# A transformer layer pair in float32: fillings for TensorE, and up projections from high and low parts

## What is computed

```python
x  = x + layernorm(attn(layernorm(x)))        # 16 heads of 16, rotary, window of 250, causal
y  = layernorm(x)                             # the second block:
z  = rmsnorm(y + attn2(y), n1)                # 16 heads, no mask, keys and values through 64 columns
shared = swiglu(z @ W_shared_in) @ W_shared_out        # 256 -> 2*512 -> 256
h      = swiglu(z @ W1_shared)                         # 256 -> 2*512
out = z + shared + sum over 8 experts of (h @ W2[e]) * w[:, e]   # top 2 of a group by a gate
x  = x + layernorm(rmsnorm(out, n2))
```

## Time and profile before

| | us |
|---|---|
| median of 3 runs | 2344.89 |
| lowest, highest | 2335.24, 2353.25 |
| profiled execution | 2316.51 |
| its span, first to last instruction | 2314.5 |
| batches 1 to 7, each (stages A to the next A) | 265.6 to 279.9 |
| batch 0 (from its A) | 239.4 |

### The profile page before, as it was taken

The page is one execution under the profiler, slowest core; times in us unless marked ns, Lnnn a source line. Parts: engine busy times, 40 slices in busy tenths (PEclk is TensorE's granted clock), DMA queues, the critical chain, the costliest instruction groups (busy, mean ns, idle before and its releaser), DMA issues.

```text
span 2314.5 us, 31755 instructions
## 1 busy us (share of the span) xinstructions
PE 2060.3 (89%) x9200; PEld 1089.0 (47%) x9200; DVE 1386.8 (60%) x4293; ACT 829.0 (36%) x1713; POOL 341.5 (15%) x647
## 2 busy tenths in 40 slices
PE   6868899998999999999899989989899998999986
PEld 4343445535364453635436353453635545354455
DVE  6457455755756466674556756575565656747454
ACT  2434424262432424334242542325233262423410
POOL 3323112101220003100031011210112101210000
PEclk8577889998998988999789998898899899889988
DMA  4003002110030101101021010211002010020212
GB/s 166 2 28 138 1 2 92 37 38 10 6 133 1 48 1 73 66 2 48 1 83 55 7 42 1 90 49 38 11 2 101 37 38 10 6 89 35 77 52 91
DMA packets 23083, 104.64 MB, mean 45 GB/s; under 512 B 3312, under 2 KB 14192, under 8 KB 18288
## 3 DMA queue, kind: packets, MB, share of 16 engines
q1 hardware_dynamic: 21168, 89.81, 10.7%
q0 software_dynamic: 1728, 12.58, 1.4%
HBM read 84.56 MB, written 16.78 MB: 44 GB/s over the span
## 4 chain that ended last, share of the span: by engine, by line
PE 70%; DVE 19%; issue 7%; ACT 3%; DMA 0%; POOL 0%; DVEq 0%; SPq 0%; POOLq 0%; ACTq 0%
PE fb L732 13%; PE fb L710 11%; PE sm L644 10%; PE ot L684 10%; PE st L670 5%; PE st L629 3%; PE st L613 3%; DVE negmax L1011 2%; DVE acc L1199 2%; DVE stats L925 2%; PE dn L652 2%; PE dn L696 2%; PE dn L613 2%; PE sm L670 1%; DVE sm L1008 1%
## 5 line engine op out<-in xcount | busy, mean ns | idle before, releaser
L535 ACT ACTIVATE probs<-st 128x512 f32<-128x512 f32 (+3 forms) x832 | 404.9, 506 | 472.9 <-PE st L670 430.0
L644 PE MATMUL sm<-k_t,q_t 48*128 48x512 f32 (+3 forms) x928 | 381.0, 483 | 101.3 <-DVE negmax L1008 49.2
L732 PE MATMUL fb<-w_r,h_r 128*128 128x512 f32 x1536 | 444.3, 426 | 13.3 <-DVE acc L1199 13.3
L1011 DVE TENSOR_REDUCE negmax<-sm 128x1 f32<-128x512 f32 x464 | 302.7, 686 | 121.8 <-PE sm L644 120.3
L644 PEld LDWEIGHTS sm<-k_t,q_t 48*128 48x128 f32 x928 | 167.7, 207 | 435.8 <-DVE negmax L1008 211.9
L670 PE MATMUL st<-q_t,k_t 64*128 64x512 f32 (+3 forms) x832 | 352.0, 477 | 13.6 <-ACT probs L535 12.0
L732 PEld LDWEIGHTS fb<-w_r,h_r 128*128 128x128 f32 x1536 | 279.0, 195 | 126.0 <-issue 60.1
L710 PE MATMUL fb<-xn_t,wup_s 128*128 128x512 f32 x512 | 321.6, 723 | 6.8 <-DVE h_s L1184 4.1
L1008 DVE CUSTOM_DVE_ANT_0 sm<-sm,mask_qk 128x384 f32<-128x384 f32 (+2 forms) x464 | 213.3, 468 | 177.9 <-PE sm L644 175.4
L684 PE MATMUL ot<-probs,v_s 128*32 128x512 f32 (+3 forms) x2048 | 273.0, 554 | 3.2 <-POOL probs L438 1.8
L670 PEld LDWEIGHTS st<-q_t,k_t 64*128 64x128 f32 x832 | 153.0, 202 | 132.0 <-ACT probs L535 85.7
(11 more groups left out here) (165 smaller groups left out, 2433.2 us busy)
## 6 DMA issues: line engine op xcount, KB each, us to landing
w_r<-w_parts SPq DMA_DIRECT2D x32, 2048.0 KB, 7.8
w_parts<-w_r POOLq DMA_DIRECT2D x4, 2048.0 KB, 8.8
x_s<-in_L_attn_query SPq DMA_DIRECT2D x8, 512.0 KB, 4.4
h_s<-in_L_ffn_W_experts POOLq DMA_DIRECT2D x8, 512.0 KB, 6.1
q_t<-rot_b SPq DMA_DIRECT2D x256, 4.0 KB
x_kept<-o_s SPq DMA_DIRECT2D x8, 512.0 KB, 3.1
xa<-x_kept SPq DMA_DIRECT2D x8, 512.0 KB, 3.9
out<-acc SPq DMA_DIRECT2D x8, 512.0 KB, 10.8
```

Source lines behind the costliest of these rows:

```text
L535: nc.scalar.activation(probs[:, n % PSLOTS, 0:hi - lo], score_bank(m)[:, 0:hi - lo], ACT.Exp, scale=float(D) ** -0.5).then_inc(s_ex, 1)
L644: mm(max_bank(w)[:, 0:hi - lo], q_t[r:r + MROW, b, t * P:(t + 1) * P], k_t[r:r + MROW, b, lo:hi], start=True, stop=True).then_inc(s_sm, 1)
L732: last = mm(fb[q % 2][:, :], h_r[:, h, m, rows], w2_r[:, k % 2, w, m, :], start=(m == 0 and n == 0), stop=(m == NH - 1 and n == 2))
L1011: return v.tensor_reduce(negmax[:, g % 2, n // GH, c:c + 1], max_bank(g * UNITS + n)[:, 0:hi - lo], AX.X, ALU.max, negate=True).then_inc(s ...
```

## The change

Three things are changed together.

**Up projections.** The moving rows and the weights are each split in a high part in f32r and the rest, and a product becomes three f32r matmuls (high x high, high x low, low x high). The weights are split once, on POOL at the start, and stored in DRAM (`wup_parts`, 4 MB). Each block n (512 KB) is loaded into a ring of four in SBUF, `wup_r`, once per batch. The rows are split by POOL in each batch (`split_rows`) into the first 32 of the 64 columns of every head of `stack`, after the fourth `stacks`. `hidden` waits for that split (`s_xl`) and for the block's load. Its steps now lie at -16 to 2 and, in the first group of E, at 4, 6, 9 and 12. SP issues `load_up` for blocks 0 to 3 of the next batch after the load of the next `x`, ahead of pair 2, and in the placings of attention 0 block 4 after the first group, 5 and 6 after the second, 7 after the third.

**Order.** Output 17 moves from B to A (after the transposes), 19 from before the third `stacks` of B to after it, 7 from I to the end of G (before PE waits for `xn`). DVE's order is unchanged.

**Fillings.** `keep_warm` is a float32 product of `ident` with 256 columns of `wout_t`, whose result nobody reads. There are 10 in each lead of attention 0, one after the transposes of `xn`, 12 in the tail, and in batch 0 one at every lead step and every second main step of both attentions and 16 in G.

```diff
-HIDDEN_AT = spread(8 * NH - len(QUIET), 10 - LEAD, -1) + QUIET
+QUIET = [g * UNITS + n for g in range(NGR) for n in ((2, 5, 8, 12) if g else (4, 6, 9, 12))]
+HIDDEN_AT = spread(8 * NH - len(QUIET), 12 - LEAD, 2) + QUIET
 OUT_HEADS = {0: ((17,), (), (18,), (19,), ()), 1: ((), (7,), (), (8,), ())}
+OUT_ROWS = {0: (17,), 1: (7,)}
+OUT_MADE = {0: ((), (), (18,), (), (19,)), 1: ((), (), (), (8,), ())}
+WARM_LEAD = [m - LEAD for m in (0, 1, 3, 4, 5, 7, 8, 9, 10, 11)]
+WARM_ROWS, WARM_FIRST_ROWS, WARM_LAST = 1, 16, 8
...
-        wup_s = sb("wup_s", [P, 2, NC, 2 * HID])
+        wup_r = sb("wup_r", [P, RING, 2, 2, NC, P], F32R)
+        xn_parts = [stack[:, w, :, 0:NC * D] for w in range(2)]
...
+            def load_up(f, n):
+                if n >= RING or not isinstance(f, int) or f > 0:
+                    sp.wait_ge(s_ub, f * N_UB + n - RING + 1)
+                sp.dma_start(wup_r[:, n % RING].bitcast(F32), wup_parts[n]).then_inc(s_wu[n % RING], 16)
+            # in place_maxima of attention 0, after group g:  blocks (4,), (5, 6), (7,), ()
+            # after the load of the next x: blocks 0 to 3 of the next batch, ahead of pair 2
...
+            def split_up(u):
+                pool.wait_ge(s_wur, 16 * (u + 1))
+                if u > 0:
+                    pool.wait_ge(s_wup, 16 * u)
+                for c in range(NC):
+                    raw = wup_raw[:, c].rearrange("p (h n q) -> p n h q", h=2, n=NH)
+                    g.tensor_copy(wup_split[:, :, 0, :, c, :], raw).then_inc(s_wuh, 1)
+                ...
+            def split_rows(f, stacks_done):
+                hi, lo = (x.rearrange("p h (c d) -> p c h d", c=NC) for x in xn_parts)
+                rows = xn_t[:, :, :].rearrange("p c (h d) -> p c h d", d=D)
+                pool.wait_ge(s_sp, stacks_done)
+                pool.wait_ge(s_fc, (f + 1) * N_FC)
+                pool.sem_inc(s_seen[1], 1)
+                g.tensor_copy(hi, rows).then_inc(s_xh, 1)
+                pool.wait_ge(s_xh, f + 1)
+                g.tensor_tensor(lo, rows, hi.bitcast(F32), ALU.subtract).then_inc(s_xl, 1)
+            split_up(0)
+            split_up(1)
+            low_parts(0, 0)
+            mask_probs(0, None)
+            low_parts(0, 1)
             load_raw(0)
             load_raw(1)
             split_pair(0)
-            low_parts(0, 0)
-            mask_probs(0, None)
-            low_parts(0, 1)
             split_pair(1)
...
                 low_parts(i, 0)
+                split_rows(i - 1, i * N_SP + 16)
                 mask_probs(i, i - 1)
...
                 if s == 0:
                     pe.wait_ge(s_gr, f + 1)
+                    pe.wait_ge(s_xl, f + 1)
...
-                product = mm(fb[half][:, :], wup_s[:, u, c, col:col + P], xn_t[:, c, :], start=(c == 0), stop=(c == NC - 1))
+                if s % 4 == 0:
+                    pe.wait_ge(s_wu[n % RING], f * N_WU + 16 * (n // RING + 1))
+                for k, (w, x) in enumerate(((0, 0), (0, 1), (1, 0))):
+                    product = mm(fb[half][:, :], wup_r[:, n % RING, w, half, c, :], xn_parts[x][:, :, c * D:(c + 1) * D],
+                                 start=(c == 0 and k == 0), stop=(c == NC - 1 and k == 2))
...
+            def keep_warm(dst, times):
+                for _ in range(times):
+                    mm(dst[:, 0:E], ident[:, :], wout_t[:, 0, :], start=True, stop=True)
...
-                        for q in OUT_HEADS[a][t]:
+                        for q in OUT_MADE[a][t]:
                             out_rows(f, q)
...
                 transpose_rows(xa, pair, s_tp)
+                if e is not None:
+                    for q in OUT_ROWS[0]:
+                        out_rows(e, q)
...
-                    for q in OUT_FIRST:
+                    for q in (*OUT_FIRST, *OUT_ROWS[1]):
                         out_rows(f, q)
+                else:
+                    keep_warm(fb[0], WARM_FIRST_ROWS)
                 pe.wait_ge(s_xn, i + 1)
                 transpose_rows(xn, pair, s_tp)
+                keep_warm(fb[0] if f is None else st[1], WARM_ROWS)
```

More of the change, by code:

```diff
@@ L45 @@
 ROWS_FROM, LOGITS_AT = 2 - LEAD, 7 - LEAD
-QUIET = [g * UNITS + n for g in range(NGR) for n in (2, 5, 8, 12)]
+QUIET = [g * UNITS + n for g in range(NGR) for n in ((2, 5, 8, 12) if g else (4, 6, 9, 12))]
 QUIET_OUT = [g * UNITS + n for g in range(NGR) for n in (2, 8, 12)]
-HIDDEN_AT = spread(8 * NH - len(QUIET), 10 - LEAD, -1) + QUIET
+HIDDEN_AT = spread(8 * NH - len(QUIET), 12 - LEAD, 2) + QUIET
 OUT_FIRST, OUT_BESIDE = range(2, 7), range(9, 16)
@@ L57 @@
 GATE_EXPS_AT = (GATES_FROM + 6, GATES_FROM + 12)
+RING = 4
 SOURCE_STEPS = 8
@@ L232, in build @@
         s_hl, N_HL = sem("hidden_low_made"), NH
+        s_xh, s_xl = sem("expert_rows_high_made"), sem("expert_rows_low_made")
+        s_wur = sem("raw_up_weights_loaded")
+        s_wuh, s_wul = sem("up_weights_high_made"), sem("up_weights_low_made")
+        s_wup = sem("up_weights_stored")
+        s_wu, N_WU = [sem(f"up_weights_loaded{k}") for k in range(RING)], 16 * 2 * NH // RING
+        wup_parts = nc.dram_tensor("wup_parts", (2 * NH, P, 2, 2, NC, P), F32, kind="Internal").ap()
         w2_parts = nc.dram_tensor("w2_parts", (PAIRS, P, 2, NH, 2 * E), F32, kind="Internal").ap()
@@ L304, in _, with place_maxima @@
                 sp.dma_start(dst, src).then_inc(s_w1, 16)
+            sp.dma_start(wup_raw, w_si.rearrange("(c p) n -> p c n", p=P)).then_inc(s_wur, 16)
             for dst, src in loads:
                 sp.dma_start(dst, src).then_inc(s_w, 16)
-            def place_maxima(i, a):
+            sp.wait_ge(s_wul, NC)
+            sp.dma_start(wup_raw, w1.rearrange("(c p) n -> p c n", p=P)).then_inc(s_wur, 16)
+            def place_maxima(i, a, f=None):
                 for g in range(NGR):
@@ L315, in place_maxima @@
                                          rot_b[m:m + 2].rearrange("p h d -> p (h d)")).then_inc(s_mr[g % 2], 16)
+                    if f is not None:
+                        for n in ((4,), (5, 6), (7,), ())[g]:
+                            load_up(f, n)
             def store(f):
@@ L350, in batch @@
                 if f is not None:
+                    for n in range(RING):
+                        load_up(i, n)
+                if f is not None:
                     load_pair(f, 2, e)
@@ L356, in _ @@
             batch(0, None, None, True)
+            sp.wait_ge(s_wup, 32)
+            for n in range(RING):
+                load_up(0, n)
             sp.wait_ge(s_w2p, 16 * PAIRS)
@@ L364, in _ @@
             x1_from_dram(B - 2)
+            for n in range(RING, 2 * NH):
+                load_up(B - 1, n)
             store(B - 2)
@@ L448, in mask_probs @@
                                 hidden_low(f, k)
+            def split_up(u):
[5 more added lines that the diff above has]
+                    g.tensor_copy(wup_split[:, :, 0, :, c, :], raw).then_inc(s_wuh, 1)
+                pool.wait_ge(s_wuh, NC * (u + 1))
+                for c in range(NC):
+                    raw = wup_raw[:, c].rearrange("p (h n q) -> p n h q", h=2, n=NH)
+                    g.tensor_tensor(wup_split[:, :, 1, :, c, :], raw, wup_split[:, :, 0, :, c, :].bitcast(F32),
+                                    ALU.subtract).then_inc(s_wul, 1)
+                pool.wait_ge(s_wul, NC * (u + 1))
+                g.dma_start(wup_parts[u * NH:(u + 1) * NH].rearrange("n p w h c q -> p n (w h c q)"),
+                            wup_split.bitcast(F32).rearrange("p n w h c q -> p n (w h c q)")).then_inc(s_wup, 16)
+            def split_rows(f, stacks_done):
[12 more added lines that the diff above has]
+            low_parts(0, 1)
             load_raw(0)
@@ L708, in hidden @@
                     pe.wait_ge(s_ht, f * N_HT + n)
-                col = half * HID + m * P
-                product = mm(fb[half][:, :], wup_s[:, u, c, col:col + P], xn_t[:, c, :], start=(c == 0), stop=(c == NC - 1))
+                if s % 4 == 0:
[3 more added lines that the diff above has]
+                                 start=(c == 0 and k == 0), stop=(c == NC - 1 and k == 2))
                 if c == NC - 1:
@@ L776, in attention @@
                         max_rows(i, a, (m + LEAD) // UNITS - 1)
+                    if f is None and (m < 0 or m % 2 == 0):
+                        keep_warm(fb[0], 1)
                     if f is not None and a == 0:
+                        if m in WARM_LEAD:
+                            keep_warm(dn, 1)
                         if m == ROWS_FROM:
@@ L883, in _ @@
                 out_rows(B - 2, q)
+            keep_warm(dn, WARM_LAST)
             experts_rows(B - 1, B - 2)
+            keep_warm(dn, WARM_LAST // 2)
             gate_logits(B - 1)
```

11 lines of the change are left out of this document (6 added, 5 removed).

## The result

The changed kernel took 2369.8 us (median of 4, 2365.7 to 2416.2), beside 2340.8 for the kernel before (median of 4): 1.011 times as long, 95% interval 1.007 to 1.016. Forecast were 2320 and a gain. Run again on a second chip it took 2392.2 beside 2326.8, ratio 1.030 (1.020 to 1.039). The two intervals don't meet, so the size of the loss differs from one set of runs to the other; its sign doesn't.

The account below looks back on a forecast made before the run. PE, 89% busy with its clock repeatedly at half speed, was taken as the bound (E also waits for DVE). Terms 12 - 31.5 + 3 - 3 + 7 - 7.5 - 4.5 = -24.5 gave median 2320, range 2255 to 2375.

Parts of the forecast that it names:

- the term for C and D: C and D, seven batches: fillings hold the clock, 35.2 us against a mean of 39.7, -4.5 a batch, -31.5 in all.
- The sign: Whole kernel: a gain was forecast, with chances of 0.42 for faster, 0.37 for same and 0.21 for slower.
- rival two: C and D: fillings do not hold the clock, -1 a batch instead of -4.5; 2345, no change; chance 0.25.
- rival three: End of B: output 19 starves PE ahead of the lead and the clock falls; 2372, slower; chance 0.14.
- The order in A and B: A and B: moved outputs 17 and 19 cost +2 us in each of six batches, +12 in all.
- Products: Up products: three f32r matmuls take 0.96 us instead of 1.12, saving 0.16 at full and 0.42 at half clock.
- E: Stage E: two products more, sixteen old ones shorter; +0.5 us a batch, +3 in all.
- G and I: Output 7 moved from I to G: transposes about 1.9 us later, I shorter by 2.3; -0.4 a batch, -3.
- Start: Start: POOL's weight splits delay the first low part from 30.31 to near 36 to 38 us; +7.
- Batch 0: Batch 0 with fillings: C +4, E -4, I -1.5, J +3, K -9, together -7.5 us.
- Tail: Tail: 96 instructions take PE 22.6 us, so DVE sets the pace; -5, and +0.5 for fillings.
- Queues and ring: DMA queues: SP moves 4 MB more a batch, blocks arrive ahead of their steps; costs nothing.

Follow-up runs that it names:

- lead_fill_new: Kernel before with new products, old order, second weight split after the first low part, fillings in leads and tail, none in batch 0: 2282.0 us, 0.972 of before.
- order_undone: Changed kernel with outputs 17, 19 and 7 back in their old places, all else as changed: 2334.3 us, 1.000 of before.
- three_fixes: Changed kernel with outputs 19 and 7 back, no fillings in batch 0 and the second weight split late: 2307.2 us, 0.994 of before.
- order_on_before: Kernel before with the three moved outputs (17, 19, 7) alone, old products, no fillings: 2384.6 us, 1.026 of before.

## Why the prediction was wrong

**The step that failed** is the term for C and D: "the return is the clock", with 3 us a batch left for a half state that comes back. At full clock the two stages take 33.1 us (batch 5 of `lead_fill_new`), 1.3 more than the 31.8 of the sum. Measured are 41.6, so the half state cost 8.5 us a batch and not 3, and the term is +2.2 against the kernel before (41.6 against 39.4), where -4.5 was forecast. No row of before showed what a lead with fillings pays; the 3 was set without one. (The sum has a slip besides: 31.8 and 3 are 34.8, not 35.2.)

What took the clock stays open, but the order isn't it, or is the smaller part. The same fillings with the old order leave C and D at 39.8 (`order_undone`), with 19 back at 40.9, with three parts mended at 39.4. Within the changed kernel the same 4.33 us of idle PE and the same half-speed `stacks` stand ahead of three leads with D at 1.00 and three with D at 0.50 to 0.70. On the kernel before the fillings held it (13.1 and 23.7 at 1.00), and in `lead_fill_new` mostly. So the premise is right in some kernels and batches and wrong in others, and the forecast took it for all.

**The sign** is the work of two terms. Products and fillings without the order come out at 1.000: that is rival two's "no change", which had 0.25, though not by its parts alone, since batch 0 is 28 us longer there and E no shorter. The order adds 3.0%, 58 us by the medians, where the sum had +12 for A and B and -3 for G and I. That is rival three's place, the end of B. Its 2372 against the measured 2370 is partly luck: A and B paid 3.2 over before and not 1.6, C and D took 41.6 and not 41.2, most of it with the order undone too, and batch 0 paid 22, which the rival had at nothing; E came out cheaper than before in that trace. It had 0.14, too little: the 5 us idle ahead of the third `stacks` stood in my own sum, as a remark without a price.

**The order in A and B**: forecast +2 a batch, measured +4.8 against the same kernel with the order undone (33.6 against 28.8). Within it 17 gained 1.1 and 19 cost 5.9; the chain to the lead was put at 7.1 us and is 8.6, because the `stacks` run at half speed after the idle.

**Products**: right in size. 0.99 for 0.96; D at full clock 18.5 us. The wait for the split is nowhere in PE's waits: the 3.39 of POOL lies beside the max units. Alone they gained 2.4%, in that trace by E's clock and not in C and D. With the split late they gained 3.8%, and in that trace it is C and D that are shorter (36.0 against 39.4) and E that is as before: where the clock lies, not the 0.16 us, decides.

**E** was to grow by 0.5 a batch and is at 58.1 at full clock, against 59.0. What it costs is the clock: 58.1 to 73.7 us in one trace.

**G and I**: forecast -0.4 together. G takes 20.3 at full clock against 18.3 in `order_undone`, the +1.9 expected, and mostly 21.8, as its clock is 0.92; I was to shorten by 2.3 and shortened by 0.4 at best (22.4 against 22.8). I counted output 7's PE time in a stage that waits for other engines.

**Start**: forecast 36 to 38 for the first low part, measured 37.07. The terms given for it (11, 6.8, 8.8, 6.8) add up to 33.4 only; the store, with POOL waiting for it, took 11.1 us from 17.67 to 28.75. B of batch 0 grew by 7.8.

**Batch 0**: forecast -7.5 beside the start's +7, measured +22.1 in all. A filling between max units takes 0.63 us at full clock (873.23 to 873.86 above), not 0.53, ten of them 1 us more in each lead. The larger error is in what the clock returns: E of batch 0 went from 0.55 to 1.00 and from 58.1 to 56.9 us, since its fillings took up what the clock gave; K was to shorten by 9 and grew by 6.

**Tail**: forecast -4.5, measured -2.0 and -3.5 in the two traces, of 125.4 us after the last projection. **Queues and ring**: nothing, as forecast.

By the profiled pair: batch 0 +22, batch 1 +5, six batches of +6.0 (A+B +3.2, C+D +2.2, E -2.6, F+G +3.1), tail -3, together 60 beside the 58.6.

**Open**: why the low stretch falls where it does from batch to batch in one and the same code, and so what took the clock of C and D; whether `three_fixes` really misses `lead_fill_new`, and why; the 2 us of idle PE in A of the kernel before and of `order_on_before`.

## What to carry to other kernels

When work is moved across a hand-over between engines, follow both in-order engines to the next point where they meet: the same matmuls, put behind a transpose, delayed copies on DVE that PE needed. Beside the fillings the moved outputs cost 3.0%, more than the 2.4% that the cheaper products gained. Fillings are to be priced by their full time and by the clock of the stages after them as well; where the low stretch only moves to a longer stage, they lose. A gain in the total is to be looked for in the stages that were changed: here 10 us of the products' 50 and 10 of the lead fillings' 36 lay in A and B, which hold nothing new. Split such a change into its parts before judging it: here one part was worth -2.4% and hid behind two that together cost 5.5%.
